# Two GNN layers on one core: gathers without a bound, the convolution's bias on VectorE, the last add on POOL

## The chip, the cores and the metric

The kernel runs on one core of one Trainium2 chip. The core's engines are TensorE (PE), VectorE (DVE), ScalarE (ACT), GpSimd (POOL) and SyncE (SP, which here only issues DMAs), beside 16 DMA engines. The metric is the device time of one execution in microseconds, as a median of several runs; lower is better.

## The reference

A graph of 6250 nodes (512 features) and 100,000 edges (src, dst), the dst skewed to small numbers. Two layers, each with a residual:

```
h = relu(layernorm(x))
x = x + GAT(h)      # 8 heads; softmax over the edges of each src, sums of feat[dst]
h = relu(layernorm(x))
x = x + L1(h)

L1: xn   = batchnorm(h)                       # scale, shift per column
    agg  = segment_sum(xn[src], dst) / max(deg, 1)
    conv = relu(agg @ W_conv + b_conv)
    attn = attention with random features over the first 256 nodes (a later node takes the row of the 256th)
    out  = batchnorm(conv + attn + h)
```

The batch norm ahead of the gather is folded: W_conv is scaled by the norm's scale, and its shift times W_conv is a row that is added for each node that has an edge (indicator of degree above 0). So conv = relu(sums / degree @ (scale * W_conv) + indicator * (shift @ W_conv) + b_conv).

## The kernel before

**Sorts and padding.** Nodes are taken in 49 tiles of 128. Each edge becomes one 32 bit key: major node, 13 bits of minor node. DVE and PE sort 128 x 1024 keys twice (by src for layer 0, by dst for layer 1). The edges of a node tile are filled up with padding to a multiple of 256 (layer 0) or 128 (layer 1); padding has all 13 minor bits set, so it reads as node 8191. `prepare` makes the keys, `slot_fields` takes the sorted ones apart: minor nodes to `minorA` or `minorB` (the rows to gather), major nodes to a one-hot column. A padding slot gets a major number outside the tile, so that its one-hot column is zero.

**Gathers.** POOL gathers 128 rows at a time with an indirect DMA: 880 of `feat_table` (2112 bytes a row) in layer 0, `gather_batch`, 16 a batch into a ring of two batches; 832 of `h1_table` (2048 bytes a row) in layer 1, `gather_row`, 8 a row into a ring of three rows. Both have a bound of N - 1 with `oob_is_err=False`: a slot with index 8191 fetches nothing, and the place keeps what it held. PE multiplies each chunk of 128 gathered rows by its one-hot matrix into PSUM (L858 in layer 0, L1624 in layer 1), DVE adds the result to the tile's sums in `acc` (L682, L1423). In layer 0 the softmax logits of the next batch need all its 16 gathers (L539, L827). ACT puts the next indices out.

**Attention.** PE, ACT and DVE pass through the heads by named steps. Between them DVE prepares the row shift @ W_conv (`shrow`) and the bias, each cut into three bf16 rows (`parts1`, L1328 and L1334), which go by way of `bias_table` in HBM to `bias_rows`, 6 rows of bf16.

**Convolution.** For each tile t: DVE divides by the degree (L1438), PE transposes (L1637), ACT copies (L1266), PE multiplies by W_conv in 4 products, 8 passes (L1645), and a fifth product of 6 rows adds the bias: 3 rows of the indicator and 3 of ones (`ind_rows`, spread by way of `ind_table`), times `bias_rows` (L1650). DVE makes y = max(psum, 0) + h (L1448). ACT keeps y and its square (L1271, L1274), POOL adds both to column sums (L1179, L1180). PE works one tile ahead; y of t waits for POOL's sums of t - 2, and the product of t for y of t - 2.

**Last loop.** For each tile DVE computes sums x scale (L1486) and adds x1 + shift (L1492), all in SBUF; POOL had added the shift to the x1 tile (L1196). SP loads x1 four tiles ahead, when a tile is out, and stores the output.

What sets the order is the program's own text on each engine, with semaphores between them.

Of the kernel before, what the change touches and what calls it, by code (L numbers as in the profile page):

```python
# [5 lines left out]
P = 128  # L6
# [33 lines left out]
NO_NODE = TILES * P + P - 1  # L40
AD_W = 14 * D
# [42 lines left out]
def build(nc, x, src, dst, W0, att_w, norm1_g, norm1_b, norm2_g, norm2_b, W_conv, b_conv, Wq, Wk, Wv, Wo, proj, out):  # L84
    with ExitStack() as ctx:
# [17 lines left out]
        ind_table = nc.dram_tensor("ind_table", (TILES, P), BF16).ap()  # L103
        bias_table = nc.dram_tensor("bias_table", (6, D), BF16).ap()
# [26 lines left out]
        iota_pad = sb("iota_pad", [P, PAD_COLS], F32)  # L131
        ones = sb("ones", [P, H], F32)
# [841 lines left out]
        shrow = ad_flat[0:1, 4 * D:5 * D]  # L974
        bcrow = ad_flat[0:1, 5 * D:6 * D]
        parts1 = rows2_flat[0:1, 512:512 + 3 * D].bitcast(BF16).rearrange("p (n d) -> p n d", n=6)
        bias_rows = keys_flat[0:6, 2 * D:2 * D + D // 2].bitcast(BF16)
        indT = wk1[0:TILES, 0:P // 2].bitcast(BF16)

        ind_rows = ad_flat[0:6, AD_W - TILES * P // 2:].bitcast(BF16)  # L980
        bn1_sd = sem("bn1_sd")
        bn1_step = sem("bn1_step")
        SHIFT_ROW = 8
        bn1_shift = sem("bn1_shift")
        bn1_ps = sem("bn1_ps")
        parts_ready = sem("parts_ready")
        bias_stored = sem("bias_stored")
# [53 lines left out]
        deg_ready = sem("deg_ready")  # L1041
        ind_ps = sem("ind_ps")
        ind_ready = sem("ind_ready")
        ind_spread = sem("ind_spread")
# [12 lines left out]
        bn2_ready = sem("bn2_ready")  # L1057
# [4 lines left out]
        out_stored = [sem(f"out_stored{n}") for n in range(4)]  # L1062
        scale2, shift2, mean2, sd2 = (ad_flat[:, (6 + n) * D:(7 + n) * D] for n in range(4))
# [24 lines left out]
        def layer1_sync(sp):  # L1088
# [6 lines left out]
            sp.dma_start(bcrow, row_of(b_conv)).then_inc(bc_loaded, 16)  # L1095
            sp.wait_ge(parts_ready, 1)
            sp.dma_start(bias_table.rearrange("n d -> (n d)").rearrange("(u c) -> u c", u=1),
                         parts1.rearrange("p n d -> p (n d)")).then_inc(bias_stored, 16)
            sp.wait_ge(bias_stored, 16)
            SPE.wait(sp, "wo")  # L1100
            sp.dma_start(bias_rows, bias_table).then_inc(bias_stored, 16)
# [6 lines left out]
            for q in range(4):  # L1108
                sp.dma_start(x1buf[:, q, :], x1_table[q * P:(q + 1) * P, :]).then_inc(x1_in[q], 16)
            sp.wait_ge(ind_ready, 2)  # L1110
            sp.dma_start(ind_table, indT).then_inc(ind_spread, 16)
            sp.wait_ge(ind_spread, 16)
            sp.dma_start(ind_rows[0:3, :], row_of(ind_table.rearrange("t n -> (t n)")).broadcast_to([3, TILES * P])
                         ).then_inc(ind_spread, 16)
# [27 lines left out]
        def layer1_gpsimd(pool):  # L1142
# [10 lines left out]
            def gather_row(r):  # L1153
                pool.wait_ge(idx3, r(1, 1))
                if r.i is None and r.c == RING1 - 1:
                    SPE.wait(pool, "aT")
                    pool.wait_ge(bias_stored, 16)
                for hf in range(2):
                    pool.wait_ge(lot1_ps, r(SB, 4 * hf + 4))
                    pool.sem_inc(hold, 1)  # L1160
                    for b in range(4 * hf, 4 * hf + 4):
                        g.indirect_dma_start(rows_l1[LOTS * r.place + b // 2][:, b % 2 * D:(b % 2 + 1) * D], None, h1_table,  # L1162
                                             bass.IndirectOffsetOnAxis(ap=idx[:, r.place, b:b + 1], axis=0),
                                             bounds_check=N - 1, oob_is_err=False).then_inc(h_arrived[r.place][hf], 16)
# [26 lines left out]
            pool.wait_ge(bn2_ready, 1)  # L1191
# [5 lines left out]
            with pool.Fori(0, QUADS) as i:  # L1197
                for q in range(4):
                    shift_x1(q, i * 16 + 16)
            shift_x1(0, 16 * (QUADS + 1))  # L1200
# [87 lines left out]
        def layer1_vector(dve, link, links):  # L1288
# [25 lines left out]
            v.tensor_tensor(shift_c, b1c, shift_c, ALU.subtract).then_inc(bn1_shift, 1)  # L1314
            dve.wait_ge(bn1_ps, 1)
            step(v.tensor_copy(shrow, psE[0:1, :]))
# [7 lines left out]
            dve.wait_ge(bc_loaded, 16)  # L1324
            for n, row in enumerate((shrow, bcrow)):
                for m in range(3):
                    last = n == 1 and m == 2
                    ins = v.tensor_copy(parts1[:, 3 * n + m, :], row)  # L1328
                    if last:
                        ins.then_inc(parts_ready, 1)  # L1330
                    else:
                        step(ins)
                    if m < 2:
                        step(v.tensor_tensor(row, row, parts1[:, 3 * n + m, :], ALU.subtract))  # L1334
# [92 lines left out]
            v.tensor_scalar(indc, acc[:, :, D], 1.0, None, ALU.min).then_inc(deg_ready, 1)  # L1427
# [13 lines left out]
            def make_y(t, q, loads, first=False):  # L1441

                dve.wait_ge(conv_ps, t + 1)
                dve.wait_ge(hc_in[q], loads)
# [35 lines left out]
            step2(v.tensor_tensor(scale2, g2row, sd2, ALU.mult))  # L1480
            step2(v.tensor_tensor(shift2, mean2, scale2, ALU.mult))
            v.tensor_tensor(shift2, b2row, shift2, ALU.subtract).then_inc(bn2_ready, 1)

            def finish(t, q, stores):
                dve.sem_inc(hold, 1)
                v.tensor_tensor(tbuf[:, q, :], acc[:, bass.ds(t, 1), 0:D].rearrange("p a d -> p (a d)"), scale2,  # L1486
                                ALU.mult).then_inc(scaled, 1)
                dve.wait_ge(scaled, t + 1)
                dve.wait_ge(shifted, t + 1)
                if stores is not None:  # L1490
                    dve.wait_ge(out_stored[q], stores)
                v.tensor_tensor(obuf[:, q, :], tbuf[:, q, :], x1buf[:, q, :], ALU.add).then_inc(out_ready, 1)  # L1492
            for q in range(4):
                finish(q, q, None)
            with dve.Fori(1, QUADS) as i:
                for q in range(4):
                    finish(i * 4 + q, q, i * 16)
            finish(TILES - 1, 0, 16 * QUADS)

        def layer1_tensor(pe):  # L1500
# [23 lines left out]
            for k in range(KD):  # L1524
                ins = pet.matmul(psE[0:1, :], shift_c[:, k:k + 1], Wc_s[:, k, :], start=(k == 0), stop=(k == KD - 1))
# [103 lines left out]
            pe.wait_ge(deg_ready, 1)  # L1629
            pet.transpose(psD[0:TILES, 0:P], indc, ident).then_inc(ind_ps, 1)  # L1630

# [496 lines left out]
```

## Time and profile before

| | us |
|---|---|
| median of 3 runs | 3712.99 (3712.64 to 3714.53) |
| the profiled execution | 3717.24 |
| its span, first to last instruction | 3715.4 |

| engine | busy us | share |
|---|---|---|
| PE | 2492.9 | 67% |
| DVE | 2669.2 | 72% |
| ACT | 963.8 | 26% |
| POOL | 2098.5 | 56% |

The stages by the timeline: first sort and dense products to about 410 us, second sort to 740, gathers of layer 0 to 1946, x1 and norms to 2132, attention to 2270, gathers of layer 1 to 3351, convolution to 3579, last loop to the end. Granted PE clock 0.876 of full speed over the span.

How to read it: a stage ends when its slowest engine or transfer does, so the busy shares are read by stage, and the wait ahead of an instruction ("<-" names what ended it) tells who is late. "issue" is idle time in which the engine waited for nothing that the profile shows.

### The profile page before, as it was taken

To read this page: it belongs to the slowest core of one execution; us is meant where nothing else is said; L and a number is where in the kernel's file an instruction comes from. 1 tells how busy PE (TensorE), PEld (TensorE's weight loads), DVE (VectorE), ACT (ScalarE), POOL (GpSimd) and SP (SyncE) were. 2 spreads that over 40 slices of the span, in tenths; PEclk is the share of its full clock that TensorE was granted. 3 is DMA by queue.
4 is the path that set the end of the run, shared out by engine and by line. 5 is a ranking of instruction groups with operands and counts; after the bars stand their busy time and mean duration, and the time that the engine had idled before them with its cause. 6 is when DMAs were issued, how large, how long until landed. Compare 5 with 4: busy or idle time off the path is not lost. (4 is left out here: it accounts for less than half of the span.)

```text
span 3715.4 us, 48525 instructions
## 1 busy us (share of the span) xinstructions
PE 2492.9 (67%) x10737; PEld 1499.5 (40%) x10738; DVE 2669.2 (72%) x4400; ACT 963.8 (26%) x3073; POOL 2098.5 (56%) x1976
## 2 busy tenths in 40 slices
PE   0699001168889888889880087877777777778950
PEld 0465001156667666667660064333333333333420
DVE  9666898768878888878889935766666666663259
ACT  4533000045555555555551320000000000002320
POOL 0000200077777777777758723777777777774555
PEclk9999555579999999999995567999999999999975
DMA  4011100077777777777619313666666666642226
GB/s 164 35 53 56 41 0 0 7 210 222 218 215 218 218 208 221 216 207 223 205 32 325 121 57 89 199 201 198 197 194 191 192 193 191 195 127 63 59 89 204
DMA packets 236188, 562.42 MB, mean 151 GB/s; under 512 B 68092, under 2 KB 68098, under 8 KB 236143
## 3 DMA queue, kind: packets, MB, share of 16 engines
q0 software_dynamic: 136960, 416.19, 38.5%
q1 hardware_dynamic: 99186, 145.76, 12.0%
q8 instruction: 16, 0.26, 0.0%
q14 instruction: 26, 0.21, 0.0%
HBM read 547.60 MB, written 54.12 MB: 162 GB/s over the span
## 5 line engine op out<-in xcount | busy, mean ns | idle before, releaser
L461 POOL DMA_INDIRECT big<-feat_table,idx x880 | 887.6, 1009 | 634.8 <-issue 591.9
L1162 POOL DMA_INDIRECT big<-h_table,idx x832 | 831.1, 999 | 369.0 <-issue 362.0
L858 PE MATMUL psA<-big,onehot 128*128 128x260 f32 x1760 | 460.6, 407 | 16.1 <-DVE big L672 13.9
L858 PE MATMUL psB<-big,onehot 128*128 128x260 f32 x1760 | 436.2, 391 | 10.3 <-DVE acc L682 6.9
L528 ACT ACTIVATE big<-big,late_weights 128x65 f32<-128x65 f32 x1760 | 434.0, 340 | 0.0
L858 PEld LDWEIGHTS psA<-big,onehot 128*128 128x128 f32 x1760 | 330.2, 198 | 105.6 <-issue 37.0
L1624 PE MATMUL psA<-big,onehot 128*128 128x512 f32 x556 | 309.1, 638 | 85.8 <-DMA big<-h_table,idx 64.1
L1624 PE MATMUL psB<-big,onehot 128*128 128x512 f32 x554 | 308.0, 638 | 77.1 <-DMA big<-h_table,idx 71.1
L1624 PE MATMUL psC<-big,onehot 128*128 128x512 f32 x554 | 307.4, 637 | 76.9 <-DMA big<-h_table,idx 69.0
L858 PEld LDWEIGHTS psB<-big,onehot 128*128 128x128 f32 x1760 | 319.8, 192 | 67.7 <-DVE acc L682 20.6
L502 ACT CAST idx<-minorB 128x8 int32 (+1 forms) x107 | 21.5, 203 | 1056.3 <-DMA big<-h_table,idx 1050.7
L1423 DVE TENSOR_TENSOR acc<-acc,psA 128x513 f32 x278 | 191.8, 690 | 128.8 <-PE psA L1626 115.0
L1423 DVE TENSOR_TENSOR acc<-acc,psB 128x513 f32 x277 | 191.1, 690 | 127.1 <-PE psB L1626 114.9
L1423 DVE TENSOR_TENSOR acc<-acc,psC 128x513 f32 x277 | 191.1, 690 | 126.7 <-PE psC L1626 114.1
L1738 POOL MEMSET acc<- 128x25480 f32 x1 | 21.3, 21331 | 365.1 <-DMA feat_table<-big 365.1
L672 DVE TENSOR_TENSOR big<-big,psD 128x1040 f32<-128x1040 f32 x168 | 204.2, 1229 | 0.0
L1906 DVE TENSOR_TENSOR big<-big 128x512 f32<-128x512 f32 x278 | 192.5, 692 | 9.6
L672 DVE TENSOR_TENSOR big<-big,psE 128x1040 f32<-128x1040 f32 x162 | 196.9, 1229 | 0.0
L1907 DVE TENSOR_TENSOR big<-big 128x512 f32<-128x512 f32 x278 | 190.4, 685 | 0.0
L2033 PE MATMUL psA<-ident_wide,big 128*128 128x128 f32 x224 | 42.5, 352 | 210.3 <-DVE big L1924 167.7
L1645 PE MATMUL psA<-big 128*128 128x512 f32 x392 | 178.6, 599 | 0.0
L2056 PE MATMUL psB<-big 128*128 128x512 f32 x392 | 177.7, 596 | 0.0
(349 smaller groups left out, 3932.7 us busy)
## 6 DMA issues: line engine op xcount, KB each, us to landing
nodes_all<-slot_nodes SPq DMA_DIRECT2D x112, 256.0 KB, 5.0
big<-feat_table,idx POOLq DMA_INDIRECT x880
big<-h_table,idx POOLq DMA_INDIRECT x832, 3.6
feat_table<-big SPq DMA_DIRECT2D x49, 264.0 KB, 2.1
x_table<-acc SPq DMA_DIRECT2D x49, 256.0 KB, 3.6
h_table<-big SPq DMA_DIRECT2D x49, 256.0 KB, 2.0
big<-h_table SPq DMA_DIRECT2D x49, 256.0 KB, 2.6
big<-x_table SPq DMA_DIRECT2D x49, 256.0 KB, 2.7
```

The costliest lines, as they stand in the source:

```text
L461: g.indirect_dma_start(ring[:, b.k, q * SB + u, :], None, feat_table, bass.IndirectOffsetOnAxis(ap=idx[:, 2 * b.k + q, u:u + 1], axis=0), ...
L528: ins = s.activation(part, part, ACT.Copy, scale=late_weights[:, at:at + 1])
L672: v.tensor_tensor(pair, pair, weight_ps[b.k][:, 2 * a * H:(2 * a + 2) * H] .rearrange("p (b h) -> p b h", h=H).unsqueeze(3).broadcast_to([ ...
L858: ins = pet.matmul(psum[:, 512 * hf:512 * hf + HALF_W], onehot[:, q, u % SB, :], ring[:, b.k, u, HALF_W * hf:HALF_W * (hf + 1)], start=(u ...
L1162: g.indirect_dma_start(rows_l1[LOTS * r.place + b // 2][:, b % 2 * D:(b % 2 + 1) * D], None, h1_table, bass.IndirectOffsetOnAxis(ap=idx[:, ...
L1423: v.tensor_tensor(d, d, lot1_sums(r, b)[:, 0:D + 1], ALU.add).then_inc(lot1_added, 1)
L1624: pet.matmul(psum[:, 0:D], onehot[:, r.q, b, :], rows_l1[LOTS * r.place + b // 2][:, b % 2 * D:(b % 2 + 1) * D], start=True, stop=True)
L1645: pet.matmul(psA[:, q * 512:(q + 1) * 512], aggT[:, q, k * P:(k + 1) * P], Wc_s[:, k, :], start=(k == 0), stop=False)
L1906: v.tensor_tensor(low, a, b, ALU.min).then_inc(sort_step, 1)
L1907: v.tensor_tensor(high, a, b, ALU.max).then_inc(sort_step, 1)
L2033: ins = pet.transpose(psA[:, b * P:(b + 1) * P], keys[:, at, b * P:(b + 1) * P], ident)
L2056: pet.matmul(psB[:, q * D:(q + 1) * D], hTbuf[:, q, k * P:(k + 1) * P], W4[:, k, :, :].rearrange("p h o -> p (h o)"), start=(k == 0), stop ...
```

## The change

It does four things.

1. Padding keys get minor values 7168 + 2p + c (p the partition, c the column, up to 255) instead of 8191. `slot_fields` takes 7168 off again, so that each padding slot asks for one of the nodes 0 to 509. For that there is an iota more on POOL at the start, an OR on DVE, and in each `slot_fields` a `tensor_tensor` of 128x1024 more. Padding is still outside every tile by its major number.
2. The gathers lose `bounds_check` and `oob_is_err=False`.
3. The bias: the product of 6 rows, its rows, tables and DMAs go. The product shift @ W_conv is made for 128 equal rows; `bias_ps` is the bias in PSUM (psD). DVE makes y in three steps instead of one.
4. The last loop: scale and shift are kept in PSUM (psB); DVE computes sums x scale, then + shift; POOL adds x1 last and waits for the x1 load and for the store that frees the output buffer.

```diff
+PAD_MINOR = 7 << 10
+PAD_SPAN = COLS // 4
...
                         for u in (2 * a, 2 * a + 1):
                             g.indirect_dma_start(ring[:, b.k, q * SB + u, :], None, feat_table,
-                                                 bass.IndirectOffsetOnAxis(ap=idx[:, 2 * b.k + q, u:u + 1], axis=0),
-                                                 bounds_check=N - 1, oob_is_err=False).then_inc(rows_arrived[b.k], 16)
+                                                 bass.IndirectOffsetOnAxis(ap=idx[:, 2 * b.k + q, u:u + 1], axis=0)).then_inc(rows_arrived[b.k], 16)
...
-            for n, row in enumerate((shrow, bcrow)):
-                for m in range(3):
-                    last = n == 1 and m == 2
-                    ins = v.tensor_copy(parts1[:, 3 * n + m, :], row)
...
-                    if m < 2:
-                        step(v.tensor_tensor(row, row, parts1[:, 3 * n + m, :], ALU.subtract))
...
-            dve.wait_ge(bias_stored, 32)
-            dve.wait_ge(ind_ps, 1)
-            v.memset(ind_rows, 1.0).then_inc(ind_ready, 1)
-            v.tensor_copy(indT, psD[0:TILES, 0:P]).then_inc(ind_ready, 1)
+            dve.wait_ge(bc_loaded, 16)
+            link(v.tensor_copy(bias_ps, bias_rows))
...
-                return v.scalar_tensor_tensor(ybuf[:, q, :], psA[:, q * 512:(q + 1) * 512], 0.0, h_in[:, q, :],
-                                              ALU.max, ALU.add)
+                y = ybuf[:, q, :]
+                v.scalar_tensor_tensor(y, shift_rows, indc[:, bass.ds(t, 1)], psA[:, q * 512:(q + 1) * 512], ALU.mult,
+                                       ALU.add).then_inc(y_step, 1)
+                dve.wait_ge(y_step, t * 2 + 1)
+                v.tensor_tensor(y, y, bias_ps, ALU.add).then_inc(y_step, 1)
+                dve.wait_ge(y_step, t * 2 + 2)
+                dve.wait_ge(hc_in[q], loads)
+                return v.scalar_tensor_tensor(y, y, 0.0, h_in[:, q, :], ALU.max, ALU.add)
...
-            def shift_x1(q, loads):
+            def add_x1(t, q, loads, stores):
+                pool.wait_ge(shifted, t + 1)
                 pool.wait_ge(x1_in[q], loads)
+                if stores is not None:
+                    pool.wait_ge(out_stored[q], stores)
                 pool.sem_inc(hold, 1)
-                g.tensor_tensor(x1buf[:, q, :], x1buf[:, q, :], shift2, ALU.add).then_inc(shifted, 1)
+                g.tensor_tensor(obuf[:, q, :], tbuf[:, q, :], x1buf[:, q, :], ALU.add).then_inc(out_ready, 1)
...
-                link(v.memset(key, (NO_NODE << SHIFT) | MINOR_MASK | KEY_BASE))
+                link(v.tensor_scalar(key.rearrange("p (a c) -> p a c", c=PAD_SPAN),
+                                     pad_keys[:, :].unsqueeze(1).broadcast_to([P, COLS // PAD_SPAN, PAD_SPAN]),
+                                     NO_NODE << SHIFT, None, ALU.bitwise_or))
...
-                link(v.tensor_copy(minor_t[:, :, :].rearrange("p b r -> p (b r)"), seg))
+                link(v.tensor_scalar(other.bitcast(I32), seg, float(PAD_MINOR), -float(PAD_MINOR), ALU.is_ge, ALU.mult))
+                link(v.tensor_tensor(minor_t[:, :, :].rearrange("p b r -> p (b r)"), seg, other.bitcast(I32), ALU.add))
```

PE in the convolution loop, where `big` is the transposed tile or the weights; before, one tile:

```order
L1637 MATMUL psC<-ident_wide,big 128x128 x4
L1641 REGISTER_ALU
L1643 REGISTER_ALU
L1645 MATMUL psA<-big 128x512 x4
L1650 ISA
L1650 MATMUL psA<-big 128x512
```

and after:

```order
L1608 MATMUL psC<-ident_wide,big 128x128 x4
L1612 REGISTER_ALU
L1614 REGISTER_ALU
L1616 MATMUL psA<-big 128x512 x4
L1604 REGISTER_ALU
```

The fifth product is gone; the rest stands as it did. DVE in the last loop, one tile before (`onehot` is the buffer of the scaled tile, the second `big` x1 or the scale):

```order
L1486 ISA
L1486 TENSOR_TENSOR onehot<-acc,big 128x512
L1488 REGISTER_ALU
L1491 REGISTER_ALU
L1492 TENSOR_TENSOR big<-onehot,big 128x512
```

and after:

```order
L1463 ISA
L1463 TENSOR_TENSOR onehot<-acc,psB 128x512
L1465 REGISTER_ALU
L1466 TENSOR_TENSOR onehot<-onehot,psB 128x512
```

Both of DVE's instructions now read one operand from SBUF and one from PSUM, and what is left of the tile stands on POOL.

## Rows read from the trace of the kernel before

**Rows 1.** Windows, gather stages: PE, PEld, DVE, ACT, POOL busy, clock, DMA, GB/s
```profile
1000.00:1500.00 500.00, 441.59 (x2529) 341.95 (x2525) 412.74 (x844) 262.90 (x960) 374.96 (x372) 0.97 0.74 215
2500.00:3000.00 500.00, 387.03 (x1153) 152.98 (x1152) 315.12 (x432) 9.78 (x48) 382.96 (x384) 1.00 0.67 195
```

**Rows 2.** Chain that ended last, shares of the span by line
```profile
by line: POOL big L1162 19.0%; issue 9.9%; PE psA L1645 4.6%; DVE onehot L1486 1.4%; DVE big L777 1.1%; PE psC L1637 0.8%; DVE acc L1423 0.7%; DMA big<-h_table,idx 0.7%; POOLq L1162 0.6%; PE psB L1624 0.5%; PE psA L1650 0.4%; PE psA L1624 0
```

**Rows 3.** Groups, window 2275 to 3348: busy us, mean ns | idle before
```profile
L1162 POOL DMA_INDIRECT big<-h_table,idx x808 | 806.1, 998 | 268.6 <-issue 261.8 <-PE psB L1626 2.4 <-PE psC L1626 2.1
```

**Rows 4.** Timeline of POOL, last gather: start, us, what [idle before]
```profile
3343.91 0.99 POOL L1162 DMA_INDIRECT big<-h_table,idx  x1 [0.30 <-issue]
```

**Rows 5.** Timeline of DVE early in the layer 1 stage
```profile
2307.07 1.22 DVE L1408 TENSOR_TENSOR onehot<-psD,nodeB 128x1024 f32<-128x1024 f32 x1
...
2315.25 1.22 DVE L1408 TENSOR_TENSOR onehot<-psD,nodeB 128x1024 f32<-128x1024 f32 x1
```

**Rows 6.** Timeline of PE in layer 0, one instruction in two batches
```profile
1894.93 0.49 PE L827 MATMUL psC<-ident_wide,look_space 128*128 128x128 f32 x2 [2.57 <-ACT look_space L539]
...
1915.73 0.49 PE L827 MATMUL psC<-ident_wide,look_space 128*128 128x128 f32 x2 [1.91 <-ACT look_space L539]
```

**Rows 7.** L1162 in POOL's queue: ns min/median/max, first, last start
```profile
L1162 POOLq MOVE  x832: 29/29/38, 2161.6 to 3328.0; - x167
```

**Rows 8.** DMA, windows 3322 to 3349 and, last row, 3200 to 3300
```profile
q0 software_dynamic: 1520, 0.01, 2.8%
...
big<-h_table,idx POOLq DMA_INDIRECT x18, 2.1
...
big<-h_table,idx POOLq DMA_INDIRECT x78, 3.6
```

**Rows 9.** Windows of the last loop and of the loop that writes x1
```profile
3593.00:3708.00 115.00, 0.00 (x0) 0.00 (x0) 111.08 (x98) 0.00 (x0) 72.82 (x49) 0.50 0.64 210
1946.00:2016.00 70.00, 0.00 (x0) 0.00 (x0) 66.92 (x90) 0.00 (x0) 69.22 (x49) 0.50 0.94 333
```

**Rows 10.** Timeline of DVE ahead of the last loop, with POOL idle
```profile
3584.45 0.69 DVE L1475 TENSOR_TENSOR big<-big 128x512 f32<-128x512 f32 x1
3585.18 0.69 DVE L1476 TENSOR_SCALAR big<-psA 128x512 f32<-128x512 f32 x1
```

**Rows 11.** Timeline of the convolution: y from PSUM, and POOL's second add
```profile
3441.28 0.69 DVE L1448 SCALAR_TENSOR_TENSOR big<-psA,big 128x512 f32<-128x512 f32 x1 [3.16 <-PE psA L1650]
...
3444.71 1.27 POOL L1180 TENSOR_TENSOR onehot<-onehot 128x512 f32<-128x512 f32 x1
```

**Rows 12.** Timeline of PE in the convolution, one period
```profile
3554.34 3.60 PE L1645 MATMUL psA<-big 128*128 128x512 f32 x8
3557.88 0.38 PE L1650 MATMUL psA<-big 6*128 6x512 bf16 x1
3558.19 0.66 PE L1637 MATMUL psC<-ident_wide,big 128*128 128x128 f32 x4
3558.68 3.60 PE L1645 MATMUL psA<-big 128*128 128x512 f32 x8
```

**Rows 13.** Timeline of DVE ahead of the convolution
```profile
3353.53 5.29 DVE L1432 MEMSET big<- 6x6272 bf16 x1 [1.36 <-issue]
```

**Rows 14.** Timeline of DVE in the attention
```profile
2176.40 0.40 DVE L1328 CAST big<-big 1x512 bf16<-1x512 f32 x1
...
2182.07 2.15 DVE L1337 TENSOR_SCALAR big<-big,alphas 128x512 f32<-128x512 f32 x4
2184.25 4.84 DVE L1343 TENSOR_REDUCE small<-acc 128x1 f32<-128x512 f32 x8
```

**Rows 15.** Timeline of ACT in the attention, its last copy of k features
```profile
2182.40 1.09 ACT L1223 COPY acc<-psB 128x512 f32<-128x512 f32 x2
```

**Rows 16.** Timeline of DVE after the second sort
```profile
725.61 1.22 DVE L1954 TENSOR_TENSOR big<-big 128x1024 f32<-128x1024 f32 x1
```

**Rows 17.** DMA issues, window 2262 to 2290: size, us to landing
```profile
big<-in_L_gnn_norm_b_dram SPq DMA_DIRECT2D x1, 256.0 KB, 5.2
```

More of the change, by code:

```diff
@@ L40 @@
 NO_NODE = TILES * P + P - 1
+PAD_MINOR = 7 << 10
+PAD_SPAN = COLS // 4
+assert N <= PAD_MINOR and 2 * (P - 1) + PAD_SPAN <= min(N, 1 << 10) and PAD_COLS <= PAD_SPAN
 AD_W = 14 * D
@@ L972, in build @@
         mean_c, var_c, scale_c, shift_c, sd_c = (vecs[:, 8 + 4 * n:12 + 4 * n] for n in range(5))
[L974 to L980, printed above, removed]
+        shift_rows, bias_rows = (ad_flat[:, (4 + n) * D:(5 + n) * D] for n in range(2))
+        shift_wide = rows2_flat[:, D:D + KD * P].rearrange("p (k m) -> p k m", k=KD)
+        bias_ps = psD[:, :]
         bn1_sd = sem("bn1_sd")
         bn1_step = sem("bn1_step")
-        SHIFT_ROW = 8
+        SHIFT_ROW = 9
         bn1_shift = sem("bn1_shift")
         bn1_ps = sem("bn1_ps")
-        parts_ready = sem("parts_ready")
-        bias_stored = sem("bias_stored")
         acc_cleared = sem("acc_cleared")
@@ L1189, in layer1_gpsimd @@
             add_y(0, LAST)
-            pool.wait_ge(bn2_ready, 1)
-            def shift_x1(q, loads):
+            def add_x1(t, q, loads, stores):
+                pool.wait_ge(shifted, t + 1)
                 pool.wait_ge(x1_in[q], loads)
+                if stores is not None:
+                    pool.wait_ge(out_stored[q], stores)
                 pool.sem_inc(hold, 1)
-                g.tensor_tensor(x1buf[:, q, :], x1buf[:, q, :], shift2, ALU.add).then_inc(shifted, 1)
-            with pool.Fori(0, QUADS) as i:
+                g.tensor_tensor(obuf[:, q, :], tbuf[:, q, :], x1buf[:, q, :], ALU.add).then_inc(out_ready, 1)
+            for q in range(4):
+                add_x1(q, q, 16, None)
+            with pool.Fori(1, QUADS) as i:
                 for q in range(4):
-                    shift_x1(q, i * 16 + 16)
-            shift_x1(0, 16 * (QUADS + 1))
+                    add_x1(i * 4 + q, q, i * 16 + 16, i * 16)
+            add_x1(TILES - 1, 0, 16 * (QUADS + 1), 16 * QUADS)
         def layer1_scalar(act, link, links, put_indices):
@@ L1479, in layer1_vector, with finish @@
             step2(v.reciprocal(sd2, sd2))
[L1480 to L1486, printed above, removed]
+            step2(v.tensor_tensor(scale_ps2, g2row, sd2, ALU.mult))
+            step2(v.tensor_tensor(shift2, mean2, scale_ps2, ALU.mult))
+            step2(v.tensor_tensor(shift_ps2, b2row, shift2, ALU.subtract))
+            def finish(t, q, first=False):
+                if not first:
+                    dve.wait_ge(out_ready, t - 3)
+                v.tensor_tensor(tbuf[:, q, :], acc[:, bass.ds(t, 1), 0:D].rearrange("p a d -> p (a d)"), scale_ps2,
                                 ALU.mult).then_inc(scaled, 1)
                 dve.wait_ge(scaled, t + 1)
[L1489 to L1492, printed above, removed]
+                v.tensor_tensor(tbuf[:, q, :], tbuf[:, q, :], shift_ps2, ALU.add).then_inc(shifted, 1)
             for q in range(4):
-                finish(q, q, None)
+                finish(q, q, True)
             with dve.Fori(1, QUADS) as i:
                 for q in range(4):
-                    finish(i * 4 + q, q, i * 16)
-            finish(TILES - 1, 0, 16 * QUADS)
+                    finish(i * 4 + q, q)
+            finish(TILES - 1, 0)
         def layer1_tensor(pe):
@@ L1524, in layer1_tensor @@
             for k in range(KD):
-                ins = pet.matmul(psE[0:1, :], shift_c[:, k:k + 1], Wc_s[:, k, :], start=(k == 0), stop=(k == KD - 1))
+                ins = pet.matmul(psE[:, :], shift_wide[:, k, :], Wc_s[:, k, :], start=(k == 0), stop=(k == KD - 1))
             ins.then_inc(bn1_ps, 1)
@@ L1644, in convolve @@
                 for k in range(KD):
[L1645 to L1652 removed]
+                    ins = pet.matmul(psA[:, q * 512:(q + 1) * 512], aggT[:, q, k * P:(k + 1) * P], Wc_s[:, k, :],
+                                     start=(k == 0), stop=(k == KD - 1))
+                ins.then_inc(conv_ps, 1)
             turn(0, 0, True)
@@ L1727, in _ @@
                          allow_small_or_imprecise_dtypes=True))
+            const(g.iota(pad_keys[:, :], [[1, PAD_SPAN]], base=PAD_MINOR, channel_multiplier=2))
             const(g.iota(iota_row[:, :], [[1, P]], base=0, channel_multiplier=0, allow_small_or_imprecise_dtypes=True))
```

58 lines of the change are left out of this document (14 added, 44 removed).

## The prediction

> **What bounds the kernel now.** First the windows of two stages: the gathers of layer 0 (1000 to 1500 us) and of layer 1 (2500 to 3000 us) [rows 1]. No engine is full there: PE 88% and 77%, DVE 83% and 63%, DMA 74% and 67%, POOL 75% and 77%. The chain that ended last names POOL all the same: 19.0% of the span on L1162, and 9.9% "issue", which is mostly the gap that stands between two gathers [rows 2]. So POOL is at its pace without being busy. The groups of the layer 1 stage say what the pace is [rows 3]: 808 gathers in 1073 us, each 998 ns, and the timeline shows the next one 0.30 us after it, all the way to the last one [rows 4]. That is 1.30 us a gather, and 808 of them are 1053 of the 1073 us. PE and DVE wait. DVE's own pace is seen right after the start of the stage, when 24 gathers had run ahead: from one one-hot (L1408) to the next are 8.18 us for 8 chunks of 128 edges, so 1.02 us a chunk [rows 5]. Layer 0 is close to the same bound: 16 gathers a batch are 20.8 us at the same pace, and from one L827 to the next are 20.8 us, of which PE sat idle 1.9 us waiting for gathered rows [rows 6]; without that it needs 18.9 us.
>
> **The gathers without bounds.** 880 + 832 gathers lose their bound. Each also loses a register move in POOL's queue (29 ns); the last move runs at 3328.0, the last gather at 3343.9, a dozen gathers later [rows 4, 7], so the queue is far ahead and the move is hidden: 0. What the test itself costs inside the 998 ns no row shows. One bound from below: the last 26 gathers of layer 1 hold padding alone, they move nothing (1520 packets and 0.01 MB in 27 us [rows 8]), and they take the same 1.00 us as those that move 256 KB [rows 4]. So no row of 128 costs POOL less for failing the test: the test is not a branch around work; it is either some cycles of each row, or nothing that can be told. From above: the gain ends where DVE's 1.02 us and PE's 18.9 us take over, 0.28 us a gather in layer 1 and 1.9 us a batch in layer 0. I take 0, because the nearest rows, with and without rows to fetch, differ by nothing; the other end is a rival below. The Trainium skill (GPSIMD Engine Reference, 3.1 Elementwise) prices a data-dependent branch on the Q7 cores at about 12 cycles an element; 128 of them would be an estimated 1.28 us, more than the whole gather takes here, so by that page too a removed branch is not the case. The Trainium skill (DMA: Bandwidth & Descriptors, Anatomy of one DMA) calls descriptor generation small, with many descriptors free before it shows; this trace disagrees, since 0.998 us of generation a gather sets the pace of two stages; by the page the gathers' cost on POOL would not matter at all, and the sum would be the same as mine.
>
> **The padding now moves data.** 12,640 of layer 0's 112,640 slots and 6,496 of layer 1's 106,496 were skipped (the counts follow from the rounding of each node tile's edges and from the rows of 1024 slots); they now fetch 26.7 and 13.3 MB. The DMA engines have room (0.74 and 0.67 busy [rows 1]), and a gather of full rows keeps POOL's pace already. What comes on top is at the end of each stage: a gather of padding alone lands 2.1 us after issue, a full one 3.6 [rows 8]. So +1.5 us for each of two stages: **+3 us** (0 to +6).
>
> **The last loop (scale, shift, x1).** Before, DVE's two instructions and POOL's one share it: 98 DVE instructions fill 111 of 115 us, mean 1133 ns, so 2.35 us a tile for 49 tiles [rows 9]. The same forms alone take 0.69 us each, one starting 0.73 us after the other [rows 10]; 1.45 us a tile. The rest is waiting for POOL's adds, with both in SBUF. Now the scale and shift lie in PSUM, so that DVE reads one SBUF operand, and POOL's add (1.27 us with none in its way [rows 11]) stands beside it. Then DMA is next: a tile moves 524 KB, and the loop that writes x1 runs at 333 GB/s with 0.94 of DMA busy [rows 9], which is 1.57 us a tile at that rate and 1.48 at full. I take 1.5: 49 x 0.85 = 41.7 saved, less 1.3 for POOL's add at the end: **-40 us**. Ends: 1.43 (the pace of the x1 loop, 70 us for 49 tiles), -44; 1.9 if x1 returns late, -21. The Trainium skill (same page, same section) gives a DMA's data time as bytes over 436 GB/s; that is an estimated 1.20 us a tile, and the loop would run at DVE's 1.45: -43 instead of -40; the 333 GB/s row decides. The Trainium skill (GPSIMD Engine Reference, 4.1 Engine selection) speaks against the move itself, a two-input add being some 2x slower there than on VectorE; the rows say 1.27 against 0.69, and the sum only needs it under 1.5.
>
> **The convolution loop.** PE is full: four-pass products start every 4.34 us (3554.34, 3558.68), and the bias product ends that period [rows 12]: it starts 3.54 us in, and the transposes 0.31 us later. Without it the transposes follow the eighth pass: 0.31 to 0.40 saved, taken 0.35: 49 x 0.35 = **-17 us** (-15 to -20). DVE gets two instructions a tile (0.73 each). Beside PE they lie free: three y steps are 2.2 us of about 4.0, and the average is one short instruction more. But y(t) waits for POOL's sums of y(t-2). From the start of y to the end of POOL's second add are 4.70 us now (3441.28 to 3445.98 [rows 11]); it becomes 4.70 + 1.5 = 6.2, up to 7.4 if the last y step, with two SBUF inputs, waits for an add of 1.27; two periods are 8.0. So PE stays the bound. The last tile pays the two steps: **+1.5**. Ahead of the loop the indicator rows go: a fill of 5.29 us on DVE stands before the first average, with 1.36 us of waiting before it [rows 13]; a copy of the bias (0.69) takes its place: **-6 us** (-3 to -8).
>
> **Attention and sorts.** Ten casts and subtractions of one row go: they run from 2176.40 to 2182.07, and the eight maxima behind them run without a gap, so DVE was late [rows 14]. Next late is ScalarE's last copy, done at 2183.49 [rows 15]; the maxima would end 0.6 later, at 2184.1 instead of 2189.1: **-5 us** (-3 to -5.7). The product for the shift has 128 rows instead of one; its copy takes as long and the widening copy of 512 is beside 14 us of other products: 0. In the sorts, each field step gets an add of 128x1024 (1.22 [rows 16]); the first lies ahead of a wait for the stores of the masks and is hidden by it, the second is not: +1.3. Each key step gets a 224 wide OR and the start an iota and an OR of 256, an estimated 0.4 us each by their width; the fill of 1024 becomes an OR of about the same length: **+3 us** (0 to +6).
>
> **Sum.** 3 - 40 - 17 + 1.5 - 6 - 5 + 3 = -60.5. The profiled execution took 3717.2 us, its span is 3715.4, the median is 3713.0: the execution is 4 us above it, the same on both sides. 3713 - 60 = **3653 us**. With every term at its end: 3637 to 3699.
>
> **The rivals.** *A gather is cheaper without its test.* 998 ns are 7.8 ns a row; if the test is some eighth of that, it is 0.1 us a gather. Then layer 1 gives 808 x 0.1 = 81 and layer 0 53 batches x 16 x 0.1 = 85 more: 3487. At most 226 + 101 = 327 more: 3326. For it: both stages stand at this pace, so nothing eats the gain at first; against it: a gather that fails every test costs the same [rows 4, 8]. *A gather is dearer.* The form without a bound is another one, and could be built in another way. Place: POOL in both stages; it decides from 60 / 1656 = 0.036 us a gather on. At 0.1 us dearer: 3653 + 166 = 3819, **slower**. Nothing in the trace speaks for it; it is the case that no row excludes. *Padding fetches few rows.* Sorted, the 76 gathers of padding alone ask for three to thirty different rows each, so 128 reads meet in one place; if each took 2.6 us it would be 76 x 1.3 = 99 more, 3752. The 2.6 is half of what the trace has for the nearest case: of two broadcasts of one 2 KB row to 128 partitions, issued together amid gathers, the later one landed in 5.2 us [rows 17]. Against it: that landing has the wait of every transfer in it (2.1 us even of an empty one), and it hits only these 76.
>
> **How the numbers follow.** Forecast (gather within 0.02 us of now) 0.47; cheaper 0.38, of which 0.10 by more than 0.13 us; dearer 0.09; padding 0.03; small terms that fail together 0.03. The range takes the forecast's own 3637 to 3699 and the cheaper gather down to 0.13 us (3653 - 105 - 110 = 3438): 3438 to 3702 leaves out 0.10 below and 0.10 above. A measurement of this kernel can tell about 0.2% (7.4 us). Faster 0.88, same 0.02, slower 0.10.
>
> **What would show it.** Gather 998 ns with a gap of 0.30 in both stages; any other number there moves the result by 1.66 us for each ns. Last loop: 49 tiles in 75 us, both DVE forms at 0.69. Convolution: 4.0 us from one first pass to the next, and no wait of DVE for POOL. First average 1.9 us after the last add. Maxima end where ScalarE's copies do. If the last loop stays above 1.9 us a tile, or the period at 4.34, those terms are wrong. I am wrong as a whole if the gather changed.

## The result and the profile after

| | us |
|---|---|
| before, median of 4 runs | 3713.76 (3712.64 to 3718.44) |
| after, median of 4 runs | 3588.26 (3586.19 to 3593.17) |
| ratio | 0.966, 95% interval 0.965 to 0.968 |
| the profiled execution of after | 3586.21, span 3584.4 |

The change gains 125 us, twice the 60 that were forecast. The lines of after answer to [rows 3] (808 gathers there, all 832 here; L1162 is now L1143, and L461 of layer 0 is L463), with mean ns of one behind the busy time:

```profile
L463 POOL DMA_INDIRECT big<-feat_table,idx x880 | 837.7, 952 | 637.6 <-issue 600.2
L1143 POOL DMA_INDIRECT big<-h_table,idx x832 | 786.5, 945 | 362.4 <-issue 299.1
```

A gather takes 946 ns (median) where it took 998. The windows of after, with the columns of [rows 1]; the first two answer to them, the third is the last loop and answers to [rows 9]:

```profile
1000.00:1500.00 500.00, 450.70 (x2612) 350.58 (x2611) 429.79 (x869) 273.06 (x997) 369.63 (x389) 0.98 0.80 237
2500.00:3000.00 500.00, 403.46 (x1201) 159.48 (x1201) 328.36 (x451) 10.18 (x50) 378.18 (x401) 1.00 0.73 210
3502.00:3577.00 75.00, 0.00 (x0) 0.00 (x0) 64.67 (x98) 0.00 (x0) 61.46 (x49) 0.50 0.92 322
```

401 gathers in 500 us are 1.247 us each, so 0.946 and the same gap of 0.30. The last loop does its 49 tiles in 75 us, with DMA 0.92 busy. The chain that ended last still names the gathers, but DVE's y steps (L1419, L1422, L1425) and ACT's square of y (L1257) have come in, answering to [rows 2]:

```profile
POOL big L1143 14%; DMA big<-h_table,idx 4%; PE psA L1616 2%; PE psC L1598 1%; PE psB L1598 1%; DVE acc L1396 1%; PE psA L1598 1%; DVE big L1425 1%; DMA big<-x_table 1%; DVE big L778 1%; DVE big L1419 1%; DVE big L1422 1%; ACT onehot L1257 0%; POOL big L1177 0%; PE psE L1572 0%
```

Where the time went, by the first and last starts of the instructions that bound each stage (us; the last four columns of runs are told below):

| stage | before | after | pad_only | gather_only | bias_on_pe_2 | both |
|---|---|---|---|---|---|---|
| up to the first gather | 739.7 | 741.2 | 742.6 | 741.4 | 743.3 | 743.4 |
| gathers of layer 0 | 1173.5 | 1125.6 | 1171.9 | 1126.1 | 1125.4 | 1126.6 |
| to the first gather of layer 1 | 249.2 | 249.7 | 249.5 | 250.7 | 252.3 | 250.2 |
| to the first one-hot (attention) | 121.7 | 114.4 | 120.6 | 121.0 | 121.2 | 114.4 |
| to the last add of layer 1 | 1066.2 | 1024.6 | 1067.6 | 1025.2 | 1025.3 | 1027.4 |
| to the first product of the convolution | 10.9 | 5.0 | 10.8 | 10.8 | 10.9 | 5.5 |
| to the start of its last y | 214.1 | 223.4 | 213.4 | 214.2 | 214.1 | 192.8 |
| to the last loop | 17.6 | 18.1 | 17.5 | 17.6 | 17.8 | 17.7 |
| last loop to the end | 122.5 | 82.4 | 121.3 | 121.0 | 83.5 | 83.0 |

The spans of the two profiled executions differ by 131.0 us (the medians by 125.5; before's execution was 4 us above its median, after's 2 below): gathers -47.9 and -41.6, last loop -40.1, attention -7.3, head -5.9, and the convolution **+9.3** where -15.5 was forecast.

What the convolution does now, two tiles of the timeline of after (start us, us, what, idle before and what ended it):

```profile
3384.03 3.70 PE L1616 MATMUL psA<-big 128*128 128x512 f32 x8 [0.35 <-ACT big L1249]
...
3388.05 0.75 DVE L1419 SCALAR_TENSOR_TENSOR big<-big,stat,psA 128x512 f32<-128x512 f32 x1 [0.93 <-PE psA L1616]
...
3388.84 0.69 DVE L1422 TENSOR_TENSOR big<-big,psD 128x512 f32<-128x512 f32 x1
...
3389.47 1.27 POOL L1160 TENSOR_TENSOR onehot<-onehot 128x512 f32<-128x512 f32 x1
3389.55 1.73 DVE L1425 SCALAR_TENSOR_TENSOR big<-big 128x512 f32<-128x512 f32 x1
...
3391.48 0.62 ACT L1254 COPY acc<-big 128x512 f32 x1 [2.94 <-DVE big L1425]
...
3392.00 0.62 ACT L1257 ACTIVATE onehot<-big 128x512 f32<-128x512 f32 x1
...
3392.53 0.57 ACT L1249 COPY big<-psC 128x512 f32<-128x512 f32 x1
...
3393.15 3.70 PE L1616 MATMUL psA<-big 128*128 128x512 f32 x8 [0.35 <-ACT big L1249]
```

PE is no longer full; its product waits for an ACT copy (L1249). That copy is of data transposed one tile earlier, so it isn't waiting for PE: it stands in ACT's queue behind the keeping of y and its square (L1254, L1257), and these wait for DVE's third y step. This closes a circle over two tiles: product 3.70, 0.32 to y, three y steps 3.23, 0.20, three ACT instructions 1.62, 0.05, the product of two tiles on: 9.12 us, 4.56 a tile. The third y step, with y and h both in SBUF, takes 1.55 or 1.73 us and ends 0.54 to 0.56 us after POOL's second add does (here at 3391.28 after 3390.74).

### The profile page after: what moved, and what is told of

Same layout as the page of the kernel before. It is cut to its first block and busy times, and to the rows that moved or that the text cites. A ratio compares the mean times of both kernels' runs of the same rounds, so it can differ in the third digit from the quotient of the medians.

```text
span 3584.4 us, 46885 instructions
## 1 busy us (share of the span) xinstructions
PE 2462.1 (69%) x10687; PEld 1488.0 (42%) x10688; DVE 2728.3 (76%) x4493; ACT 964.0 (27%) x3073; POOL 1994.4 (56%) x1977
## 5 line engine op out<-in xcount | busy, mean ns | idle before, releaser
L463 POOL DMA_INDIRECT big<-feat_table,idx x880 | 837.7, 952 | 637.6 <-issue 600.2
L1143 POOL DMA_INDIRECT big<-h_table,idx x832 | 786.5, 945 | 362.4 <-issue 299.1
L859 PE MATMUL psA<-big,onehot 128*128 128x260 f32 x1760 | 451.9, 401 | 16.0 <-DVE big L673 13.8
L859 PEld LDWEIGHTS psB<-big,onehot 128*128 128x128 f32 x1760 | 318.4, 191 | 64.4 <-DVE acc L683 17.6
L1396 DVE TENSOR_TENSOR acc<-acc,psB 128x513 f32 x277 | 191.0, 690 | 118.8 <-PE psB L1600 105.9
L1705 POOL MEMSET acc<- 128x25480 f32 x1 | 21.3, 21332 | 365.4 <-DMA feat_table<-big 365.4
```

The lines of the kernel that those rows point to most:

```text
L859: ins = pet.matmul(psum[:, 512 * hf:512 * hf + HALF_W], onehot[:, q, u % SB, :], ring[:, b.k, u, HALF_W * hf:HALF_W * (hf + 1)], start=(u ...
L1396: v.tensor_tensor(d, d, lot1_sums(r, b)[:, 0:D + 1], ALU.add).then_inc(lot1_added, 1)
```

## The experiments

Their theory on the gathers is that the test on the index costs 52 ns each; on the convolution that the circle above sets 4.56.

One plain word on the numbers: the four runs of the first group ran on another chip, on which the kernel before takes 4136.84 us; it grants TensorE a lower clock in the gather stages (last section). They are read by durations of instructions and by the convolution stage, whose granted clock is 1.00 there too.

**bound_back**, the changed kernel with the bound on both gathers again:

```diff
-  bass.IndirectOffsetOnAxis(ap=idx[:, r.place, b:b + 1], axis=0)).then_inc(h_arrived[r.place][hf], 16)
+  bass.IndirectOffsetOnAxis(ap=idx[:, r.place, b:b + 1], axis=0),
+  bounds_check=N - 1, oob_is_err=False).then_inc(h_arrived[r.place][hf], 16)
```

(and the same for the gathers of layer 0)

> The changed kernel with the bound put back on both kinds of gather; padding still asks for the nodes 0 to 509. Theory (the test on the index costs POOL 52 ns a gather): gathers back from 946 to 998 ns, the gap between them still 0.30, layer 0 longer by 48 us and layer 1 by 42, 3588 + 90 = 3678. Rival (the gather is cheaper because each slot now has a row to fetch, so that no slot is treated apart): 946 ns stay, 3588. Second rival (the register move ahead of each gather was not hidden): 946 ns, but the gap longer by some 0.05 us, 3678 again by another way.

Measured (ns min/median/max of one, first and last start):

```profile
L1144 POOL DMA_INDIRECT big<-h_table,idx x832: 992/998/1047, 2409.4 to 3733.2; - x167
```

Gathers take 998 ns again, though every slot has a row to fetch. The second rival is out with the first: the duration itself moved, and not the gap. The time was 4100.17 (4089.42 to 4111.23), which says nothing against 3588 on this chip.

**pad_only** and **gather_only**, on a chip like the first, settle the time: the kernel before with part 1, and with parts 1 and 2.

> The kernel before with the first part alone: padding asks for the nodes 0 to 509, the bound stays, and so do the bias and the last loop of before. Theory (the padding adds bytes where DMA has room, three microseconds of landing and the instructions of the sorts): +0 to +6, 3716 to 3722, gathers 998 ns. Rival (a row that is fetched costs POOL less than a row that fails the test, and this is the gain): gathers 946 ns, 90 us faster, 3626.

Measured: 3720.51 beside 3715.21 of before (ratio 1.0011, interval 1.0001 to 1.0020), gathers 998 ns. The padding costs 5 us (0.4 to 7 by the interval), and the expected 0 to +6 holds.

```profile
L1166 POOL DMA_INDIRECT big<-h_table,idx x832: 992/998/1255, 2164.0 to 3344.2; - x167
```

> The kernel before with the first two parts: padding as above, and no bound on either gather. Theory (the test costs 52 ns a gather and is all of this part's gain): gathers 946 ns, layer 0 at 1125 and layer 1 at 1025, 90 us under pad_only, 3628. Rival (some of the gain needs the other parts): over 3640.

Measured: 3631.55 (ratio 0.977, 0.976 to 0.979), gathers 946 ns, 89 us under pad_only. The form without the bound is the whole gain of this part: 880 x 52 ns are 45.8 us, and layer 0 is 45.8 shorter than in pad_only; 808 x 52 ns are 42.0, and layer 1 is 42.4 shorter. What inside the bounded form takes the 52 ns, the test itself or something that comes with it, no run tells; below, "the test" stands for both.

```profile
L1165 POOL DMA_INDIRECT big<-h_table,idx x832: 942/946/1256, 2118.2 to 3256.5; - x167
```

**probe**, six gathers of each kind at the end of the changed kernel:

```diff
+  for k in range(0, 6):
+      g.indirect_dma_start(*places(128, k)).then_inc(probed, 16)
+  for k in range(6, 12):
+      g.indirect_dma_start(*places(128, k), bounds_check=N - 1, oob_is_err=False).then_inc(probed, 16)
...
```

> The changed kernel with 36 more gathers of rows of layer 1 at its end, 6 of each kind: 128, 64 and 32 rows, without and with the bound. Theory A (the test is some cycles of each row): the difference is 52 ns at 128 rows, 26 at 64, 13 at 32. Theory B (the test is some instructions once a gather): 52 ns at each width. In both, the rest is a fixed part and a part by the row; from 128 to 64 it tells how much of 946 ns is which. About 42 us more in all.

The lines of the six loops (ns min/median/max, first and last start): 128, 64 and 32 rows, without and with the bound in turn.

```profile
L1190 POOL DMA_INDIRECT acc<-h_table,idx x6: 946/946/971, 3581.4 to 3587.7; - x6
L1192 POOL DMA_INDIRECT acc<-h_table,idx x6: 994/998/1022, 3589.0 to 3595.5; - x6
L1194 POOL DMA_INDIRECT acc<-h_table,idx x6: 897/903/920, 3596.8 to 3602.9; - x6
L1196 POOL DMA_INDIRECT acc<-h_table,idx x6: 934/941/955, 3604.1 to 3610.3; - x6
L1198 POOL DMA_INDIRECT acc<-h_table,idx x6: 859/864/882, 3611.6 to 3617.4; - x6
L1200 POOL DMA_INDIRECT acc<-h_table,idx x6: 904/904/921, 3618.6 to 3624.6; - x6
```

The test costs 52, 38 and 40 ns: theory A would want 26 and 13 at the smaller widths, theory B 52 throughout, and the truth, from six gathers of each kind, is nearer to B: some 40 once a gather and little by the row. The same holds of the gather: a quarter of the rows (32) takes 91% of the time (864 of 946). The one execution took 3637.63 us, 46 more than the changed kernel in after_again, below.

**bias_on_pe** and, on a chip like the first, **bias_on_pe_2**: the changed kernel with its bias part undone.

> The changed kernel with its bias part undone: the product of 6 rows and its tables are back, DVE makes y in one step. Theory (the convolution loop of the changed kernel lost time, since PE now waits at 4.56 us a tile where it was full at 4.34): loop 9 to 10 us shorter, period 4.34; head of the loop 6 longer, attention 7 longer; 3588 - 10 + 13 = 3591. Rival (the bias part gained what its arithmetic says, 17 + 6 + 5 - 1.5, and the 25 us that are missing were lost elsewhere): 3588 + 27 = 3615.

Measured: 4129.46 us (before, on this chip, 4136.84); the convolution 213.5 us beside 223.6 of bound_back on the same chip, head 10.9 beside 5.4. The theory's stage numbers hold.

> The changed kernel with its bias part undone, as bias_on_pe, on a chip of this call. Theory: loop 10 us shorter (213.5 instead of 223.3), head 5.5 longer, attention 6 to 7 longer: the changed kernel's 3590 + 2, so the bias part is worth nothing in sum. Rival (the part gains as forecast, 26 us): 3615.

Measured: 3595.99 (3591.16 to 3597.05), against 3588.26 and 3591.20 of the changed kernel in other groups. The part gains 5 to 8 us, not 26: convolution +9.3, head -5.9, attention -6.8, the rest in small differences ahead of the gathers. A little more than the +2 of the theory, far from the rival's 3615.

**act_first**: the transposed tile is copied ahead of keeping y.

```diff
-                    turn_out(i * 2 + (q + 1), 1 - q)
+                    turn_out(i * 2 + (q + 2), q)
                     keep_y(i * 2 + q, q)
```

(and the same for the tiles ahead of the loop and behind it)

> The changed kernel with one order changed: on ScalarE the copy of the transposed tile t + 2 stands ahead of keeping y(t), instead of behind it. Theory (the loop turns in a circle over two tiles: product 3.70, 0.32 to y, three y steps 3.23, ScalarE keeps y and its square 1.25, then copies the transposed tile 0.62, then the product of two tiles on; 9.12 for two): the circle is cut, PE's own 4.0 is left, 0.56 x 47 = 26 us less, 3562. Rival (POOL's sums or DVE's own load set 4.56): nothing changes, 3588.

**y_in_psum**: the second y step writes PSUM.

```diff
-                v.tensor_tensor(y, y, bias_ps, ALU.add).then_inc(y_step, 1)
+                v.tensor_tensor(psA[:, q * 512:(q + 1) * 512], y, bias_ps, ALU.add).then_inc(y_step, 1)
...
-                return v.scalar_tensor_tensor(y, y, 0.0, h_in[:, q, :], ALU.max, ALU.add)
+                return v.scalar_tensor_tensor(y, psA[:, q * 512:(q + 1) * 512], 0.0, h_in[:, q, :], ALU.max, ALU.add)
```

> The changed kernel with the second y step writing PSUM, so that the third reads PSUM and h instead of y and h, both in SBUF. Theory (the third step stands still while POOL adds, because both its operands are in SBUF): third step 0.69 instead of 1.55 to 1.73, circle 9.12 - 0.95 = 8.17, period 4.08, 3588 - 0.48 x 47 = 3565. Rival (the third step is long for its operation, maximum and add, not for its operands): 1.55 stays, 3588. Second rival (POOL's sums or PE set the period): third step 0.69, period 4.56 all the same, 3588.

Measured: 4106.90 and 4113.34 us; the convolution 205.1 and 205.0 where 223.6 stands beside them, and from the first product to the last 4.16 us a tile in both (the 4.23 that is expected of them below counts the passes of the last product in). Each gains 18, neither all that was expected, so both edits cut something and something else held. In act_first it was DVE, as its timeline shows, with PE's waits for the average (L1412; us in total, times, longest) below:

```profile
3902.95 1.37 DVE L1428 SCALAR_TENSOR_TENSOR big<-big 128x512 f32<-128x512 f32 x1
3903.73 1.72 POOL L1160 TENSOR_TENSOR onehot<-onehot 128x512 f32<-128x512 f32 x1
3904.24 1.49 DVE L1412 TENSOR_SCALAR big<-acc,stat 128x512 f32 x1
...
3905.79 0.66 PE L1611 MATMUL psC<-ident_wide,big 128*128 128x128 f32 x4 [0.26 <-DVE big L1412]
```
```profile
PEld psC L1611 <- DVE big L1412: 38.0, 45, 1.4
```

POOL's add takes 1.72 where it takes 1.27 alone, and the average behind the y step takes 1.49 where it takes 0.47, as in 17 of the 49 tiles; the transposes wait for it. In y_in_psum the third step is 0.69 and what is left is the circle through ACT:

```profile
3918.57 3.69 PE L1616 MATMUL psA<-big 128*128 128x512 f32 x8 [0.27 <-ACT big L1249]
...
3926.84 1.55 PE L1616 MATMUL psA<-big 128*128 128x512 f32 x3 [0.26 <-ACT big L1249]
```

8.27 for two tiles; the theory had 8.17.

**both** edits together, with **after_again**, the changed kernel on the same chip:

> The changed kernel with both edits of the convolution: ScalarE copies the transposed tile ahead of keeping y, and the second y step writes PSUM. Each alone came to 4.23 us a tile and 205 us for the loop. Theory (act_first is held by DVE, whose third step and average stand still while POOL adds, 158 us busy in 180; y_in_psum by the circle through ScalarE, 8.27 for two tiles): with both nothing is left but PE, 4.0 a tile, loop 195, 28 us under the changed kernel. Rival (PE itself needs 4.2 with the four transposes): 205 again, 18 under the changed kernel.

> The changed kernel itself, as the base of the runs beside it. On the chip of the four runs so far the kernel before takes 4137 us instead of 3713, and the granted clock in the gather stages is 0.77 to 0.91 where it was 0.96 to 1.00. Theory (there PE sets the pace of both gather stages, so the 52 ns a gather are worth nothing): if this chip is like that one, the gather stages last as long as with the bound (1416 and 1223), and the whole is 30 us under before, from the last loop (40), attention and head (13), less the convolution (9), near 4107. Rival (the gain of 90 us is there on any chip): 4137 - 125 = 4012.

Measured: after_again 3591.20 (this chip was like the first: before 3715.77), so its theory was not put to the test and the rival's 4012 neither; the ratio of 0.967 is the first result again. both: **3564.86** (3563.03 to 3565.57; ratio 0.959, 0.958 to 0.961), 26 us under it. Its convolution:

```profile
3370.37 3.60 PE L1619 MATMUL psA<-big 128*128 128x512 f32 x8
...
3371.61 1.26 POOL L1160 TENSOR_TENSOR onehot<-onehot 128x512 f32<-128x512 f32 x1
3371.92 0.69 DVE L1428 SCALAR_TENSOR_TENSOR big<-psA,big 128x512 f32<-128x512 f32 x1
...
3374.24 3.60 PE L1619 MATMUL psA<-big 128*128 128x512 f32 x8
```

3.87 us from one product to the next (3.91 over the loop, whose first tile takes longer), PE without a gap, and the third step not moved by POOL's add beside it. The convolution of 223.3 became 192.8 us. This version beats both kernels.

**rows_in_sbuf**: scale and shift of the last loop in SBUF, POOL adds x1 last as in the changed kernel.

```diff
-            step2(v.tensor_tensor(scale_ps2, g2row, sd2, ALU.mult))
+            step2(v.tensor_tensor(scale2, g2row, sd2, ALU.mult))
```

(and the same for the shift and for both places where DVE reads them)

> The changed kernel with scale and shift of the last loop kept in SBUF, as before, while POOL still adds x1 last. Theory (DVE and POOL stand still for each other when DVE has both operands in SBUF): a tile costs 0.69 + 0.69 + 1.27 = 2.65 one after the other or about the 2.38 of before, last loop 117 to 130 instead of 82, 35 to 48 us more than the changed kernel. Rival (the gain of the last loop came from POOL's place behind DVE's two steps, not from PSUM): 82 stays.

Measured: 3630.64, 39 us over after_again; last loop 118.8 instead of 83.3, which is 35.5. The rest lies in stages that the edit doesn't touch (3 us each in both gather stages and the attention of the profiled execution), unexplained.

```profile
3542.19 0.68 DVE L1463 TENSOR_TENSOR onehot<-acc,big 128x512 f32<-128x512 f32 x1
...
3542.56 1.43 POOL L1177 TENSOR_TENSOR big<-onehot,big 128x512 f32<-128x512 f32 x1 [0.84 <-DVE onehot L1466]
3542.91 1.64 DVE L1466 TENSOR_TENSOR onehot<-onehot,big 128x512 f32<-128x512 f32 x1
```

The shift takes 1.64 beside POOL's add, and 0.69 from PSUM. Moving the last add to POOL alone gives next to nothing (118.8 beside 121.0 to 122.5 of the kernels with the last loop of before); the place in PSUM gives 35.5 of the last loop's 39.

**one_row**: all padding asks for node 0.

```diff
-            const(g.iota(pad_keys[:, :], [[1, PAD_SPAN]], base=PAD_MINOR, channel_multiplier=2))
+            const(g.iota(pad_keys[:, :], [[0, PAD_SPAN]], base=PAD_MINOR, channel_multiplier=0))
```

> The changed kernel with all padding asking for node 0 instead of the nodes 0 to 509. Theory A (padding costs by its bytes alone): no difference. Theory B (128 reads of one row of HBM meet in one place; 73 gathers of layer 0 and 26 of layer 1 hold padding alone): each such gather takes longer to land than 3.7 us, and the end of each gather stage grows; if 2.6 us each sets the pace there, 99 x 1.35 = 134 us more at most.

Measured: 3632.37, 41 us over after_again: layer 0 +18, from its last gather to the first of layer 1 +12, layer 1 +13. The DMA issues of the last 40 us of layer 1's gathers, here and (second line) of after: x count, median us to landing.

```profile
big<-h_table,idx POOLq DMA_INDIRECT x26, 9.1
```
```profile
big<-h_table,idx POOLq DMA_INDIRECT x24, 3.5
```

Theory B holds, at a third of its upper end: 128 reads of one row do meet. Over 510 rows, as in the change, landing is 3.5 us.

## Why the prediction was wrong

**Gathers, taken 0: the step that failed first.** The argument was that gathers of nothing but padding, which fail the test in every row, take the same 998 ns [rows 4, 8]. True, but both kinds of row go through the test; no row of before stood without it, so they could not price it, and a value at one end of the open range was taken as if the rows had chosen it. bound_back and gather_only give 52 ns, and probe shows that it is mostly paid once a gather. By the prediction's own 1.66 us for each ns that is -86 instead of 0, which its second case ("cheaper", 0.38, worked out for 0.1 us) covers in kind. "Some cycles of each row" was wrong too. The register move was hidden, as said.

**Convolution, -17 and +1.5: the step that failed second.** Forecast was 4.0 a tile and "PE stays the bound"; it is 4.56. Only one circle had been followed, y to POOL's sums, with 6.2 to 7.4 us against 8.0. The longer one goes y, ACT's keeping, and ACT's next copy behind it in the queue, back to PE. In the trace of before it stands in these lines:

```profile
3441.51 3.60 PE L1645 MATMUL psA<-big 128*128 128x512 f32 x8
...
3445.72 0.69 DVE L1448 SCALAR_TENSOR_TENSOR big<-psA,big 128x512 f32<-128x512 f32 x1 [3.11 <-PE psA L1650]
...
3447.66 0.56 ACT L1266 COPY big<-psC 128x512 f32<-128x512 f32 x1
```

It takes 6.71 us (3441.51 to 3448.22) of the 8.68 of two tiles; less the 0.31 of the bias product and with 2.54 of y steps more (3.23 for 0.69) it is 8.94, over 8.0 already. Of these 2.54 one us is the third step's wait for POOL, which the prediction had seen as possible; without it the circle would be 7.9, just under 8.0. The saving itself was there: in the run both, where only PE is left to set the pace, it is 3.87 us a tile, so the product's going was worth 0.47 a tile where 0.35 was taken, and the stage is 21.3 under before. The Trainium skill (SBUF — State Buffer, SBUF: two separate sides) calls the port pair of VectorE and GpSimd an exclusive lock that is held for a whole instruction, against a VectorE instruction with two SBUF inputs or in a two-port mode. The traces agree: the third step ends 0.55 us after the add that it overlaps, it is 0.69 with one input from PSUM, and in act_first POOL's add, when it came second, was the longer one (1.72). The average, with one SBUF tensor, took 1.49 beside an add instead of 0.47; by the page it would have to be in a two-port mode. Its 0.47 where a TENSOR_SCALAR from PSUM takes 0.69 [rows 10] fits that, but no run here shows the mode.

**Last loop, -40:** right, -40.1, with 75 us for 49 tiles and both DVE forms at 0.68 to 0.69; rows_in_sbuf shows that the reason was right too. POOL's adds start 1.51 us apart, and 21 of them waited for x1 (9.4 us), so the loads hold the pace above DVE's 1.45, as forecast:

```profile
L1177 POOL TENSOR_TENSOR big<-onehot,big 128x512 f32<-128x512 f32 x49 | 61.9, 1267 | 26.8 <-DVE onehot L1466 16.1 <-DMA big<-x_table 9.4
```

The trace doesn't bear out the estimate of 1.20 us a tile by the Trainium skill (DMA: Bandwidth & Descriptors, Anatomy of one DMA): the loop moved 322 GB/s with DMA 0.92 busy, which would be 350 at full, or 1.50 us a tile.

**Head, -6:** -5.9. The lines that answer to [rows 13], after:

```profile
3255.55 0.69 DVE L1396 TENSOR_TENSOR acc<-acc,psA 128x513 f32 x1 [0.28 <-PE psA L1600]
...
3257.91 0.69 DVE L1404 COPY psD<-big 128x512 f32<-128x512 f32 x1
3258.64 0.88 DVE L1409 TENSOR_SCALAR big<-acc,stat 128x512 f32<-128x512 f32 x2
```

The first average starts 2.4 us after the last add ends (1.9 forecast).

**Attention, -5:** -7.3 over the stage. The lines that answer to [rows 14, 15]:

```profile
2129.36 2.15 DVE L1310 TENSOR_SCALAR big<-big,alphas 128x512 f32<-128x512 f32 x4
2131.54 4.84 DVE L1316 TENSOR_REDUCE small<-acc 128x1 f32<-128x512 f32 x8
```
```profile
2133.18 1.14 ACT L1206 COPY acc<-psB 128x512 f32<-128x512 f32 x2
```

The maxima end at 2136.4, 2.1 us behind the last copy (2134.3). From the first gather of layer 1 on, they end 6.8 us earlier than before, and the last copy, which the prediction held fixed, 3.3 us earlier: the copies were not next late, DVE still is.

**Padding and sorts, +3 and +3:** together 5.3 in pad_only, right in size. How it splits isn't shown: ahead of the first gather stand 2.9 of it there (1.5 in after), and its gather stages differ from before by -1.6 and +1.4, so the landing's two times 1.5 can't be told from noise. The case of hot rows, forecast at 0.03, didn't come over 510 rows; one_row shows that its mechanism exists, with 41 us for one row. The count of 76 gathers of padding alone was short: they are 99, 73 in layer 0 and 26 in layer 1.

**The sum.** With the gathers at -86 the forecast would be 3567; with the convolution stage at +9.3 instead of -15.5 it is 3592. Measured 3588. The two misses point opposite ways, so the second hid 25 us of the first. The upper end was added up wrongly: every term at its dear end gives 3685, not 3699 (nor 3702), which changes nothing here.

## What to carry to other kernels

A price that no row isolates is not 0 because two rows that both contain it are equal; take it as open, and give its middle or measure it by leaving it out. Where an engine is in lockstep, follow every circle back to it through the queues: an instruction that is ready stands behind one that waits, and two more steps on DVE came back to PE by way of ACT. Between VectorE and GpSimd, putting one of VectorE's two operands into PSUM was worth, for each instruction of 128x512 that ran beside an add of GpSimd, 0.86 us (1.55 to 0.69) and 0.95 (1.64 to 0.69), at two places of this kernel.

## What the hardware showed beside that

A gather of 128 rows by an indirect DMA costs POOL 0.95 us and the next starts 0.30 later; 32 rows still cost 0.86 and 0.30, so fewer rows a gather save next to nothing, and the bound is 0.04 to 0.05 of it.

The chip of the first group granted TensorE less in the gather stages: windows of act_first there (columns as above), beside 0.98 and 1.00 in after.

```profile
1200.00:1700.00 500.00, 388.25 (x2056) 307.80 (x2057) 343.30 (x692) 214.78 (x782) 291.35 (x307) 0.89 0.66 186
...
2900.00:3200.00 300.00, 231.90 (x608) 90.46 (x606) 165.10 (x225) 5.29 (x26) 192.31 (x203) 0.86 0.63 177
```

Two of layer 1's passes take 1.10 us at a granted clock of 1.00 and 2.08 at 0.50, the levels of 2.4 and 1.2 GHz. But the clock isn't the first thing that goes wrong there. A stretch of act_first, with DVE's waits of this kind between 2600 and 3000 us (us in total, times, longest) below:

```profile
2644.57 0.17 PE L1603 MATMUL psB<-one_b,onehot 128*128 128x1 bf16 x1
...
2645.57 1.10 PE L1601 MATMUL psA<-big,onehot 128*128 128x512 f32 x2
...
2649.38 0.69 DVE L1399 TENSOR_TENSOR acc<-acc,psB 128x513 f32 x1 [4.10 <-issue]
...
2650.13 1.16 PE L1601 MATMUL psB<-big,onehot 128*128 128x512 f32 x2 [3.45 <-DVE acc L1399]
...
2653.64 2.08 PE L1601 MATMUL psC<-big,onehot 128*128 128x512 f32 x2 [2.35 <-DVE acc L1399]
```
```profile
DVE acc L1399 <- remote: 82.8, 27, 4.9
```

PE's sum in psB is done at 2644.7, DVE adds it only at 2649.4, PE stands still meanwhile for want of a free place, and only then come its slow passes. The trace names no engine of this core for these pauses of DVE ("remote", or "issue"); in the same stage of after there is no "remote" at all. So PE's clock can be a consequence of the pauses as well as a cause of time lost, and no run parts the two. The gathers no longer set the pace there: bound_back, with gathers of 998 ns, took 1416 us for layer 0 and 1223 for layer 1, and the kernels with 946 ns took 1433 to 1445 and 1232 to 1244 (mean clock over the span 0.824 against 0.816 and 0.817). On such a chip the 90 us of the gathers, the larger part of this change's gain, are not to be had. The changed kernel itself wasn't run there; by act_first and y_in_psum, each plus the 18 us that its edit saved, an estimate for it is 4125 to 4132, which is 5 to 12 under before. Why that chip's executions pause and slow down stays open.
